# Attention by tiles: in one tile of four, one relu slot moves from VectorE to ScalarE

## What is computed

```python
def _rho_signed_sqrt(x):
    return jnp.sqrt(jax.nn.relu(x) + EPS_RHO) - jnp.sqrt(jax.nn.relu(-x) + EPS_RHO)
q = jnp.einsum('bnc,ac->bna', X, Wq)
k = jnp.einsum('bnc,ac->bna', X, Wk)
Vy = jnp.einsum('bnc,dc->bnd', X, Wy_w) + Wy_b
e = jax.nn.relu(_rho_signed_sqrt(q[:, :, None, :] + k[:, None, :, :]))
scores = jnp.einsum('bija,a->bij', e, Wphi)
m = jnp.max(scores, axis=-1, keepdims=True)
ex = jnp.exp(scores - m)
denom = jnp.sum(ex, axis=-1)
part1 = jnp.einsum('bij,bjc->bic', ex, Vy)
Ew = jnp.einsum('bij,bija->bia', ex, e)
```

## Time and profile before

| | us |
|---|---|
| median of 3 runs (lowest, highest) | 4859.86 (4846.12, 4863.34) |
| the profiled execution, its own time | 4867.8 |
| its span | 4865.9 |
| attention of layer 1, some 1.2 to 4.15 ms in the span | 60% of it |
| VectorE busy over the span | 3918.4 |
| ScalarE busy over the span | 3425.8 |
| TensorE busy over the span | 4393.9 |

### The profile page before, as it was taken

How to read it: one execution, slowest core, us unless ns; L and a number is a source line. 1 busy time by engine, 2 the same in 40 slices (tenths; PEclk the granted TensorE clock), 3 DMA queues, 4 the chain that set the end, 5 groups by cost and what they waited for, 6 DMA issues and landing times.

```text
span 4865.9 us, 84113 instructions
## 1 busy us (share of the span) xinstructions
PE 4393.9 (90%) x28586; PEld 2319.2 (48%) x28586; DVE 3918.4 (81%) x6582; ACT 3425.8 (70%) x2394; POOL 3119.4 (64%) x2716
## 2 busy tenths in 40 slices
PE   8898977887999999999999999999999999899998
PEld 3333333564444444444444444444444444677777
DVE  2889885535999999999999999999999999222225
ACT  3223212224999999999999999999999998444443
POOL 2676662433777777777777777777777775343333
PEclk9788877899999999999999999999999999999999
DMA  6000001353000000000000000000000001100002
GB/s 224 0 0 1 1 1 66 127 175 109 3 2 2 4 2 2 19 3 2 3 3 2 18 4 2 2 4 2 12 5 2 2 4 46 63 17 9 17 26 87
DMA packets 70878, 130.76 MB, mean 27 GB/s; under 512 B 8279, under 2 KB 46647, under 8 KB 66160
## 3 DMA queue, kind: packets, MB, share of 16 engines
q1 hardware_dynamic: 61552, 106.21, 6.4%
q0 software_dynamic: 9216, 23.17, 1.3%
HBM read 74.66 MB, written 61.03 MB: 28 GB/s over the span
## 4 chain that ended last, share of the span: by engine, by line
DVE 36%; issue 23%; PE 13%; POOL 6%; ACT 5%; DVEq 1%; POOLq 1%; DMA 0%; another core or an unknown queue 0%; ACTq 0%; SPq 0%
DVE e_slots L811 23%; DVE e_slots L768 5%; PE banks L2313 5%; POOL g_l L2443 3%; ACT e_slots L599 2%; DVE ew L811 2%; POOL e_slots L695 2%; PE banks L465 2%; PE banks L1662 1%; POOL e_slots L701 1%; DVE half_max L775 1%; ACT L620 1%; ACT e_slots L590 1%; PE banks L1716 1%; PE banks L302 1%
## 5 line engine op out<-in xcount | busy, mean ns | idle before, releaser
L811 DVE CUSTOM_DVE_ANT_0 e_slots<-e_slots,banks 128x1024 f32<-128x1024 f32 x2048 | 2388.8, 1215 | 52.8 <-PE banks L506 45.8
L599 ACT ACTIVATE e_slots<-e_slots 128x4096 f32<-128x4096 f32 x512 | 1851.7, 3623 | 94.9 <-POOL e_slots L701 71.3
L506 PE MATMUL banks<-ex_parts,sel 128*128 128x512 f32 x4096 | 1481.1, 448 | 174.8 <-DVE ew L811 127.9
L695 POOL TENSOR_SCALAR e_slots<-k,qt 128x1024 f32<-128x1024 f32 x889 | 988.2, 1122 | 593.4 <-DVE e_slots L768 510.2
L465 PE MATMUL banks<-e_slots,w_score 128*32 128x256 f32 x16384 | 1192.6, 393 | 80.0 <-ACT e_slots L599 78.8
L506 PEld LDWEIGHTS banks<-ex_parts,sel 128*128 128x128 f32 x4096 | 633.4, 189 | 895.6 <-DVE ew L811 756.2
L701 POOL TENSOR_SCALAR e_slots<-e_slots,qt 128x1024 f32<-128x1024 f32 x889 | 987.4, 1123 | 51.1 <-POOL e_slots L695 25.5
L465 PEld LDWEIGHTS banks<-e_slots,w_score 128*32 128x32 f32 x16384 | 394.0, 109 | 723.8 <-issue 409.8
L590 ACT ACTIVATE e_slots<-k,qt 128x1024 f32<-128x1024 f32 x508 | 564.8, 1136 | 2.1 <-DVE ew L811 1.5
L2443 POOL TENSOR_TENSOR g_l<-tmp,g_h 128x512 fp32r<-128x512 f32 x192 | 258.7, 1347 | 421.7 <-ACT g_h L2410 288.4
L768 DVE TENSOR_SCALAR e_slots<-k,qt 128x1024 f32<-128x1024 f32 x635 | 431.7, 747 | 0.0
(11 more groups left out here) (361 smaller groups left out, 4856.3 us busy)
## 6 DMA issues: line engine op xcount, KB each, us to landing
stage<-in_h SPq DMA_DIRECT2D x16, 1024.0 KB, 4.9
moe_slots<-empty_slot SPq DMA_DIRECT2D x1, 10320.0 KB, 36.6
slots<-moe_slots SPq DMA_DIRECT2D x8, 1290.0 KB
moe_out<-empty_slot SPq DMA_DIRECT2D x1, 8192.0 KB, 56.6
two_rows<-moe_out SPq DMA_DIRECT2D x16, 512.0 KB, 5.8
stage<-in_w SPq DMA_DIRECT2D x6, 1024.0 KB, 6.7
w_down<-in_w_down SPq DMA_DIRECT2D x1, 4096.0 KB, 15.2
x_between<-x_tokens SPq DMA_DIRECT2D x8, 512.0 KB, 3.7
```

What stands on the lines that cost most here:

```text
L506: ins = nc.tensor.matmul(spread[n % 2][:, half * W:(half + 1) * W], c_["sel"][:, half, n, :], ex_parts[:, par, :], start=True, stop=True)
L599: nc.scalar.activation(e_slots[:, par, four, :], e_slots[:, par, four, :], ACT.Sqrt, bias=EPS_RHO).then_inc(sqrt_done, 1)
L695: nc.gpsimd.tensor_scalar(e_slots[:, par, n, :], k2[:, :], FLT_MAX, qt[:, par, 1, place(n):place(n) + 1], ALU.min, ALU.max).then_inc(z_cla ...
L811: nc.vector.tensor_tensor_reduce(out=e, in0=e, in1=spread[n % 2], scale=1.0, scalar=0.0, op0=ALU.mult, op1=ALU.add, accum_out=ew[:, q, pla ...
```

## The change

In the tile that ScalarE prepares in its step of q = 0 (it is a tile with q = 1: tiles 5, 9, ... 125, 31 of the 128), the relu of slot 13 is made by ScalarE, after its relu 14 and ahead of root 3. VectorE, which would make it at the end of its tile of q = 3, leaves it out there and makes four slots instead of five; its relu of slot 12 then counts for two on `z_v`, so that the counts of those who wait stay as they were. The new relu has a semaphore of its own, `z_x`, on which ScalarE waits itself ahead of root 3, and VectorE once in each batch before it overwrites k.

```diff
+    X_SLOT = 13
...
+            def fourth_relu(t, par, freed, count):
+
+                act.wait_ge(xb_freed, freed + (X_SLOT + 3))
+                act.wait_ge(qt_ready, t + 1)
+                nc.scalar.activation(e_slots[:, par, X_SLOT, :], k2[:, :], ACT.Relu,
+                                     bias=qt[:, par, 0, place(X_SLOT):place(X_SLOT) + 1]).then_inc(z_x, 1)
+                act.wait_ge(z_x, count + 2)
...
-            def late_roots(t, par, freed):
+            def late_roots(t, par, freed, fourths=None):
                 sqrt(t, par, 2)
                 relu(t, par, 14, freed)
+                if fourths is not None:
+                    fourth_relu(t, par, freed, fourths)
                 sqrt(t, par, 3)
...
-                step(tg * GT + GT, 0)
+                step(tg * GT + GT, 0, fourths=tg)
...
+                dve.wait_ge(z_x, b * NG)
...
-                                        ALU.add, ALU.max).then_inc(z_v, 1)
+                                        ALU.add, ALU.max).then_inc(z_v, 2 if for_two else 1)
...
-                            z(t + 2, par, m, t * NP)
+                            if q != GT - 1 or m != X_SLOT:
+                                z(t + 2, par, m, t * NP, q == GT - 1 and m == X_SLOT - 1)
```

More of the change, by code:

```diff
@@ L368, in adaln_kernel @@
             "ex", "part", "ex_parts", "ex_t", "ew", "negmax", "half_max"))
+        z_x = sem("z_by_act_of_fourth")
         spread = [bank2(2), bank2(4)]
@@ L631, in turned, with step @@
                 nc.scalar.activation(ex_t_of[:, :, :, q, :], turned_ex, ACT.Copy).then_inc(ext_copied, 1)
-            def step(t, q, done=None):
+            def step(t, q, done=None, fourths=None):
                 par = q % 2
@@ L639, in step @@
                     normed(done)
-                late_roots(t + 1, 1 - par, (t - 1) * NP if not isinstance(t, int) or t else None)
+                late_roots(t + 1, 1 - par, (t - 1) * NP if not isinstance(t, int) or t else None, fourths)
                 first_root(t + 2, par, t * NP)
@@ L760, in next_batch, with z @@
                 dve.wait_ge(kq_taken, b + 1)
-            def z(t, par, n, freed):
+            def z(t, par, n, freed, for_two=False):
                 if Z_BY[n] != "V":
@@ L2535, in _ @@
             primed = [lnc, lno]
-            primed += [xg_stored, ext_copied, att_x, exp_done, parts_done] + [xb_freed, xb_freed]
+            primed += [z_x, xg_stored, ext_copied, att_x, exp_done, parts_done] + [xb_freed, xb_freed]
             primed += [rg_mm, hn_lo, xo_done, g1_done, g2_done, g3_done, glu_u, w3_mm, xr_done, rw3_mm] + [xo_free, xo_free] + [lo_done] * N_TMP + xr_stored
```

## The result

The changed kernel took 4878.28 us (median of 7 runs, 4873.09 to 4884.89), against 4853.42 (7 runs, 4846.12 to 4863.34) for the kernel before: the ratio is 1.0048, 95% interval 1.0036 to 1.0059. It is slower, by about half a percent. The profiled execution took 4881.88 us. (The time before is of seven runs here, the three known ahead of the prediction and four more.)

The account below looks back on a forecast made before the run. VectorE was taken to set the pace (595.28 of 600 us busy), ScalarE 3% behind. Terms -7.4 + 36 - 6.4 = +22 us, put on the median 4859.86, gave 4882 us; range over the cases 4846 to 4898.

Parts of the forecast that it names:

- The relu on VectorE: VectorE's relu left out 31 times at 0.664 us each: 20.6 us if everything it needs came as much earlier.
- the cap at slot 2 of q = 0: VectorE waits there for spread 2 until some 2041.20, so the gain is capped at 0.24 us a group.
- 1.19 us on ScalarE: Further relu adds 1.04 us, later start of root 3 adds 0.15; 0.66 is covered, 0.53 delays root 0 and root 1.
- Slot 2 of q = 1: Delayed root 1 lets VectorE be early by only 0.24 us there, not 0.66, with a wait of 0.42.
- the first term: Gain from VectorE's omitted relu, capped at slot 2 of q = 0 and q = 1: 31 x 0.24 = 7.4 us.
- The gap ahead of spread 0 at q = 1: TensorE's standstill there grows from 0.35 to 1.11 us, so its clock was expected to fall at q = 1.
- The falls: TensorE's clock drops to 0.50: 24 of 31 groups at q = 1 cost 36 us; four fewer at q = 3 return 6.4.
- Rival 1: Clock stays up at q = 1, so only the 7.4 us gain remains: 4852 us; chance 0.27.
- Rival 3: ScalarE becomes the bound, its relu of 1.19 us replacing one of 0.66: +16 us, 4876; chance 0.07.
- Rival 2: VectorE gets the full 20.6 us: 4839 us, or 4826 if the falls at q = 3 go too; chance 0.08.
- Rival 4: Clock falls at q = 1 in every group at full price, 31 x 1.66 = 51 us: 4904 us; chance 0.08.

Follow-up runs that it names:

- e3: Kernel before with VectorE leaving slot 13's relu out in one tile of four and no engine making it: 4854.75 us, ratio 0.9996.
- e5: Changed kernel with ScalarE's relu 13 ahead of relu 14 and the wait for `z_x` behind both: 4857.55 us, ratio 1.0020 to the kernel before.
- e9: Changed kernel with two spare matmuls on TensorE, only behind spread 1 of q = 1: 4853.32 us, ratio 1.0004 to the kernel before.
- e1: Changed kernel with four spare matmuls at q = 1, two ahead of spread 0 and two behind spread 1: 4853.92 us, ratio 1.0003 to the kernel before.
- e8: Changed kernel with relu 13 ahead of relu 14 and spare matmuls at q = 1 and q = 3: 4835.66 us, ratio 0.9972 to the kernel before.

## Why the prediction was right

Forecast were 4882 us and a ratio of 1.0046; measured were 4878.28 and 1.0048. The direction and the mechanism, falls of the clock at q = 1, are the forecast ones. Several sizes were off, in both directions, and that the total came so close is in part luck: the terms of the sum, as the profiled executions have them, come to half of the forecast.

- *The relu on VectorE, 0.664 us, and the cap at slot 2 of q = 0.* Right: the wait there was forecast at 0.42 and came out at 0.44, and e3 shows the 0.22 that are left when nothing else waits.
- *1.19 us on ScalarE, 1.04 and 0.15.* Right on both parts, shown apart by e5.
- *Slot 2 of q = 1, capped at the same 0.24.* Not seen: in groups without a fall the step there is 1.66 as before. The term failed because a wait stood ahead of it that the working left out. Root 0 is not only in front of root 1; the first score piece of the tile after next stands behind spread 12 on TensorE and ahead of spread 13, and needs root 0. TensorE waits there 0.49 us, and slot 13 loses 0.20. So the first term is not 7.4 us of gain but none: 90.82 against 90.81 in a group, where 90.57 was forecast. Whether the cap at q = 1 would have held was not tried, since VectorE never came there early enough to meet it.
- *The gap ahead of spread 0 at q = 1.* Forecast 1.11 us, measured 0.46. Since TensorE had already stood still for root 0, its work ahead of spread 0 ended later; most of the idle time that was forecast in one piece is there in two, 0.49 and 0.46. And e9 shows that closing part of the third gap is enough to keep the clock. What holds is the claim on which the forecast rested, that TensorE's idle time around the start of q = 1 becomes enough for a fall.
- *The falls.* Forecast 24 at q = 1 at 1.5 us and four left at q = 3; measured 17 at 1.35 and one. The sum, 36 - 6.4 = 30, was 23 - 11.5 = 11.5 in the profiled execution. Against that stands the missing gain of 7.4. The total of +22 us against the profiled execution was 14.1 there (4881.88 against 4867.8); against the medians it was 24.9. The hit on the median owes its closeness to that: the forecast sum was put on a median of before, and the profiled execution, whose falls it counted, lay above that median.
- *Rival 1*, no falls at q = 1, is e1 in effect: 1.0003 and not the 7.4 us of gain that it promised, for the reason above. *Rival 3*, ScalarE as the bound, does not hold as it was put: in e8, with the relu on it and the clock up, the group is shorter than before. But its lateness is not free either: it takes 0.2 of the relu's 0.66 us at slot 13 (90.82 against e3's 90.59). *Rival 2* falls with e3: even where ScalarE has no further work, 0.22 us a group come back and not 0.66. *Rival 4* falls by the count, 17 of 31.

## What to carry to other kernels

When an engine is 97% busy and next in line, ask for each piece of its work who else waits for it, and follow all of them: here root 0 was wanted by exp, by root 1 and by a score piece 12 slots on, and the one left out took the gain. Look at TensorE's clock in the places where it waits briefly for others: here half a microsecond more of waiting cost 1.35 us a time in half of the turns, and 0.38 us of spare matmuls saved it. A gain of a fraction of a microsecond in a loop can't be judged by the time alone as long as the falls change in number: compare turns of the loop that have none, and time the loop in the trace apart from the other stages.

## What the runs showed that was not expected

- The falls keep a distance. Where turns of the loop that follow each other have one at the same place, these falls begin 92.16 us apart by the granted clock, in every trace and whatever the turns last. How many follow each other goes with how near the turn with a fall comes to that. In the kernel before it lasts 92.41 to 92.47, and they come only in pairs; in e9 92.33 to 92.40, and they come singly and in pairs; in e1 92.29 to 92.36, in threes; in e3 92.20 to 92.26, five, five and four in a row. In the changed kernel it lasts 92.13 to 92.22, and each of the four runs of falls goes on to the end of its batch, six groups in the longest. Below 92.16 they break off again: in e5, at q = 1, it lasts 92.01 to 92.03, and they come four, one and two in a row. So e3, whose turns are 0.22 us shorter, had more falls, and they gave its gain back. That the length of the turn is the reason is read from these lengths; no run set the length on purpose to try it.
- The falls at q = 3 were fewer where there were many at q = 1: one with 17, three with 14, nine with 7 (e5), and six, six and eight with none (e1, e9, before). This is of one profiled execution each. What e1 and e9 take away at q = 1 comes back in part at q = 3. Why was not tried.
- Gaps of 0.5 us can be enough, if several come close together. Before, with 0.35 and 0.50 at q = 1 and none for root 0, no group fell; with 0.36, 0.47 and 0.52 (e5) 7 of 31 did; with 0.49, 0.46 and 0.52 (the changed kernel) 17 did. 0.38 us of matmuls whose results nobody reads prevented all of them. The same gaps stand in the groups that did not fall, so they are not the whole condition.
- Instructions of a sequencer behind a wait have a price of their own: on ScalarE they start 0.07 to 0.08 us apart, and two of them made the difference between 0.26 and 0.11 us.
